# A fused token block on Trainium2: the normalised final rows written by ScalarE straight into the payload, and turned there by identity matmuls

## The reference, cut to what matters

```python
h = (emb2[hash2] + emb3[hash3] + emb4[hash4]) / 4          # three gathers of 64 values a token
x = layernorm(h)
h = h + x + layernorm(linear_attention(x)) @ Wo + bo       # phasor features, running sums over the sequence
xf = layernorm(h)                                          # the "final rows"
node = 0
for level in range(8):                                     # a tree of 255 nodes, per token
    score = xf . w1s[node] + b1s[node]
    out += (xf @ w2s[node] + b2s[node]) * gelu(abs(score))
    node = 2 * node + 1 + (score > 0)
return h + out
```

## Time and profile before

| what | us |
|---|---|
| median of 3 runs | 322.69 (322.09 to 326.11) |
| profiled execution, its own time | 326.45 |
| its span in the profile | 324.5 |
| busy, PE / DVE / ACT / POOL | 217.1 / 206.7 / 144.7 / 220.8 |
| mean granted clock of TensorE | 0.847 of 2.4 GHz |

### The profile page before, as it was taken

How to read it: one execution, slowest core, us unless ns; L and a number is a source line. 1 busy time by engine, 2 the same in 40 slices (tenths; PEclk the granted TensorE clock), 3 DMA queues, 4 the chain that set the end, 5 groups by cost and what they waited for, 6 DMA issues and landing times.

```text
span 324.5 us, 6230 instructions
## 1 busy us (share of the span) xinstructions
PE 217.1 (67%) x1973; PEld 144.8 (45%) x1978; DVE 206.7 (64%) x864; ACT 144.7 (45%) x309; POOL 220.8 (68%) x217
## 2 busy tenths in 40 slices
PE   1300555687585887586625959999999999986230
PEld 1200253546363755364412434666666667655120
DVE  5915163849596979697995502857888877864050
ACT  0003657466565657567102015545665665610230
POOL 5777777777777777777246665107877778775774
PEclk9999959557969569969975875999999999999555
DMA  4116252434334331111001122222531010102400
GB/s 140 20 28 235 54 208 48 180 73 151 110 114 117 102 89 28 38 49 51 17 33 41 49 79 89 63 98 78 146 109 15 13 17 12 16 14 65 132 7 3
DMA packets 12574, 23.80 MB, mean 73 GB/s; under 512 B 6213, under 2 KB 8452, under 8 KB 11581
## 3 DMA queue, kind: packets, MB, share of 16 engines
q1 hardware_dynamic: 4478, 16.92, 15.4%
q0 software_dynamic: 8064, 6.49, 9.6%
HBM read 17.09 MB, written 7.40 MB: 75 GB/s over the span
## 4 chain that ended last, share of the span: by engine, by line
POOL 30%; PE 25%; issue 19%; DVE 16%; DMA 5%; ACT 4%; DVEq 0%; POOLq 0%; SPq 0%; ACTq 0%
POOL pages L316 22%; PE sc L760 7%; POOL out L355 5%; PE mm L657 3%; POOL out L362 3%; ACT xb L453 2%; DMA pages<-emb,idx 2%; PE hs L718 2%; DMA pages<-slots 2%; PE yp L734 2%; PE mm L734 1%; DVE bn L937 1%; DVE xfin L980 1%; DVE gr L1137 1%; PE hs L636 1%
## 5 line engine op out<-in xcount | busy, mean ns | idle before, releaser
L316 POOL DMA_INDIRECT pages<-emb,idx x96 | 95.3, 992 | 32.5 <-issue 28.4
L355 POOL DMA_INDIRECT out<-pages,roi x64 | 70.1, 1096 | 34.8 <-issue 19.2
L323 POOL DMA_INDIRECT slots<-xov,idx x32 | 32.0, 1001 | 21.0 <-DVE idx L929 12.5
L760 PE MATMUL sc<-scratch,wf 128*64 128x204 f32 (+2 forms) x448 | 41.7, 302 | 0.0
L1102 DVE TENSOR_TENSOR scratch<-mm,feat 128x408 f32<-128x408 f32 x38 | 22.0, 579 | 13.0 <-PE sc L760 8.8
L760 PEld LDWEIGHTS sc<-scratch,wf 128*64 128x64 f32 (+1 forms) x448 | 24.7, 136 | 9.6 <-issue 5.0
L1102 DVE TENSOR_TENSOR scratch<-yp,feat 128x408 f32<-128x408 f32 x38 | 22.0, 579 | 6.5 <-PE yp L734 6.4
L1129 DVE SCALAR_TENSOR_TENSOR g<-s,cw,ge 128x102 f32<-128x102 f32 x20 | 6.4, 318 | 21.8 <-ACT ge L469 21.8
L657 PE MATMUL mm<-sel,tri 128*128 128x512 bf16 x65 | 19.0, 446 | 0.7 <-issue 0.6
L552 PE MATMUL mm<-cw,feat 128*128 128x128 f32 x32 | 8.0, 398 | 16.9 <-ACT feat L404 16.9
L453 ACT COPY xb<-xq 64x408 f32<-64x408 f32 x19 | 9.3, 489 | 21.4 <-PE xq L705 21.4
(11 more groups left out here) (227 smaller groups left out, 572.3 us busy)
## 6 DMA issues: line engine op xcount, KB each, us to landing
wf<-nodes SPq DMA_DIRECT2D x3, 1376.0 KB
slots<-wf SPq DMA_DIRECT2D x2, 1657.5 KB, 6.0
pages<-slots SPq DMA_DIRECT2D x8, 414.4 KB
wov<-turns SPq DMA_DIRECT2D x16, 176.0 KB
pages<-emb,idx POOLq DMA_INDIRECT x96, 2.4
wf<-nodes SPq DMA_DIRECT2D x1, 1312.0 KB
cw<-small SPq DMA_DIRECT2D x1, 1031.5 KB, 4.8
out<-pages,roi POOLq DMA_INDIRECT x64
```

Of the source, the lines that this page charges most:

```text
L316: pool.indirect_dma_start(emb[:, t, j, :], None, table, bass.IndirectOffsetOnAxis(idx[:, j, t:t + 1], 0)).then_inc(g_emb[g], 16)
L323: pool.indirect_dma_start(slots, bass.IndirectOffsetOnAxis(idx1[:, t:t + 1], 0), pay[:, t, :], None, bounds_check=SLOTS - 1, oob_is_err=Fa ...
L355: pool.indirect_dma_start(rows_out, bass.IndirectOffsetOnAxis(roi[:, n:n + 1], 0), xs[:, n, D:TOKEN], None, bounds_check=B * T - 1, oob_is ...
L760: last = pe.matmul(zps[half(h), page(first - 2 * h, count)], weights, z[0:rows, c, page(first, count)], start=(c == 0), stop=(n in final))
```

## The change

The tile `xfin` is gone. DVE no longer forms the normalised final rows; it hands over `ryf`, a copy of the four columns of `ry`, and `nbf` = -mean x ry. ACT's `payload` writes the rows itself, with four activations of 128x64 in place of one copy of 128x256. PE's `turn_h` waits for ACT's payload (`a_pay`) and no longer for DVE (`d_xf`), reads the rows from the payload (stride of 130 values per tile), and turns each tile by an fp32 matmul with the identity as the moving operand: four matmuls, 64 columns of weights each, instead of two transposes of 128 columns.

```diff
@@ sb tiles
-        nbias = sb("nbias", [P, GT])
+        nbias, nbf, ryf = (sb(n, [P, GT]) for n in ("nbias", "nbf", "ryf"))
-        xfin = sb("xfin", [P, GT, D])
@@ ACT, payload(g)
                 act.wait_ge(d_xf, g + 1)
                 act.wait_ge(g_clear, 2)
-                act.copy(pay[:, tiles(g), 0:D], xfin[:]).then_inc(a_pay, 1)
+                for t in range(GT):
+                    ins = act.activation(pay[:, g * GT + t, 0:D], h2[:, g * GT + t, :], ACT.Identity, bias=nbf[:, t:t + 1], scale=ryf[:, t:t + 1])
+                ins.then_inc(a_pay, 1)
@@ PE, turn_h(g)
-                pe.wait_ge(d_xf, g + 1)
+                pe.wait_ge(a_pay, g + 1)
                 if g:
                     pe.wait_ge(a_fT, g)
                     pe.wait_ge(d_bits, g)
-                for p in range(HP):
-                    last = pe.transpose(hps[:, tile(p)], xfin[:, 2 * p:2 * p + 2, :].rearrange("q t d -> q (t d)"), ident)
+                for t in range(GT):
+                    last = pe.matmul(hps[half(t % 2), tile(t // 2)], pay[:, g * GT + t, 0:D], ident, start=True, stop=True)
                 last.then_inc(p_hT, 1)
@@ DVE, layernorms(a, r, f)
                     if f:
-                        dve.wait_ge(p_hT, f)
                         dve.wait_ge(a_pay, f)
-                    for t in range(GT):
-                        ins = dve.tensor_scalar(xfin[:, t, :], h2[:, f * GT + t, :], mv[:, c + t, 0:1], ry[:, c + t:c + t + 1], ALU.subtract, ALU.mult)
-                        if t < GT - 1:
-                            put(ins)
-                        else:
-                            ins.then_inc(d_xf, 1)
+                    put(dve.tensor_copy(ryf[:], ry[:, c:c + GT]))
+                    dve.scalar_tensor_tensor(out=nbf[:], in0=mv[:, c:c + GT, 0], scalar=-1.0, in1=ry[:, c:c + GT], op0=ALU.mult,
+                                             op1=ALU.mult).then_inc(d_xf, 1)
```

## The result

The changed kernel takes 338.45 us (median of 4 runs, 337.87 to 339.14); the kernel before, run beside it, 324.4 (322.09 to 326.12). The ratio is 1.0439, 95% interval 1.0351 to 1.0527. Medians here are over all runs of a kernel, while each ratio compares the fast runs of the two kernels alone, so the two can say different things by a per cent or two. The forecast was 327.3 with a range to 331.6: the direction is right, but the measured loss of 14 us is three times the forecast 4.6. Its profiled execution took 338.2 us, its span is 336.4, against 326.45 and 324.5 before. The last scatter, which stood at 180.61, stands at 193.85, so the first stage lost 13.2 us; the rest of the span even gained 1.3.

A forecast was written before the change was run, and what follows sets the result against it. POOL's gathers feed passes 0 to 7; passes 7 to 10 are one chain through DVE, ACT and PE. Passes 5 and 6 leave 0.8, passes 7 to 10 add 1.85, 0, 1.05, 0.9: +4.6 on 322.69 gives 327.3 us, range 323.6 to 331.6.

The forecast's parts named there:

- DVE: DVE's layernorms: four L980 operations go, two small ones come at 0.3 us, leaving DVE 0.6 us ahead.
- ACT: ACT's payload: four activations in 1.44 us replace a copy of 0.39, holding ACT 1.0 us longer a pass.
- PE: turn_h: four partly overlapping matmuls cost 0.2 us more than two transposes at the high clock, 0.4 at the low.
- The new wait: turn_h waits for ACT's payload behind centre: xT +1.85 us at the high clock, about +1.7 at the low.
- The slack taken from the gathers: Passes 3 to 6: gather waits hide +1.8 each in 3 and 4, and 2.64 of 3.5 in 5 and 6.
- Pass 9: Tail of the first stage: later payload and turn_h delay L636 and then the bits, +1.05 us.
- pass 10: Last pass, at the low clock: fT at 175.1 instead of 174.21, +0.9 us.
- that delay goes into hidden, tanh, L398 and L915 without cover: Chain behind xT in a pass with centre: the delay of +1.85 us (+1.7 at low clock) carries on in full.
- Pass 8: Pass without centre: attend 0.2 us later, bits earlier, projection starts within 0.1 of before, so 0.
- 8.95 assumed: Centre to xT in passes 3 to 7: delays of +1.8, +1.8, +1.7, +1.8 and +1.85 us.
- The rival that named the cause: PE idle before turn_h: passes 4 and 6 stay at low clock, 2.2 us a lost rise, 331.0 us; chance 0.24.
- Its sign: Clock rival's mark: first stage ends more than 7 us later, with PE's clock at 0.50 in passes 4 and 6.

The follow-up runs named there:

- the fill: Changed kernel with eight idle-filling products on PE ahead of turn_h's wait for the payload: 463.06 us, 1.037 of the kernel before; again 457.57, 1.020.
- without the hand-over: Kernel before with DVE writing rows into the payload, ACT's copy gone, four identity matmuls turning them behind DVE: 444.58 us, 1.001; with four fills 447.65, 0.999.
- changed_again: The changed kernel run once more, unaltered, in the second batch of experiments: 466.63 us, 1.038 of the kernel before.
- before_again: The kernel before, unchanged, run for its trace in the third batch: 441.1 us (1 run).
- act_four: Kernel before with payload by ACT's four activations, DVE still making xfin and PE's transposes kept: 459.98 us, 1.029; again 459.15, 1.021.
- wait_pay: Kernel before with one wait changed, turn_h waiting for ACT's payload copy instead of DVE's xfin: 458.16 us, 1.020 of the kernel before.
- order: Changed kernel with only ACT's and PE's order altered, turn_x ahead of payload and turn_h, node_scores last: 465.75 us, 1.037 of the kernel before.

## Why the prediction was wrong

**Right.** DVE: L980 to L986 is 0.14 us apart, the two small operations cost no more than the 0.3 assumed. ACT: four activations in 1.42, assumed 1.44. PE: +0.2 and +0.5, assumed 0.2 and 0.4, overlapping. The new wait: 3.87 us from centre to xT at the high clock, assumed 1.97 + 1.85 = 3.82. The slack taken from the gathers: 6.3 us against 3.6 + 2.64 = 6.2. Pass 9 cost 1.4 (1.05 forecast) and pass 10 0.8 (0.9): nbf and the bits are at 176.01 and 180.54, then 184.62 and 189.15, where L980 and the bits stood at 164.98 and 168.12, then 172.18 and 175.90.

**Wrong: the step "that delay goes into hidden, tanh, L398 and L915 without cover".** It carried the delay and took the stretch itself as unchanged. That stretch grew by 5.5 us over passes 3 to 7, because PE ran it at 1.2 GHz. Pass 8, put at 0, cost 1.6 (nbf at 164.69, 9.5 behind L980 of before; one pass later 11.0): there the clock was low, and the projection took 1.92 us for 1.08 in the kernel before:

```profile
170.26 1.92 PE L645 MATMUL yp<-wpd,yT 128*128 128x256 f32 x4
```

Together this is 7.1 of the 8.6 us by which the first stage's +13.2 exceeds the +4.6 of the forecast. Of the rest, 1.2 are centre to xT (+10.1 against 8.95 assumed): in passes 3 and 4 it took 4.60, which is +2.6 and +2.5 where +1.8 was assumed, again at the low clock, while pass 5 added 0.5 less than assumed; and 0.3 are pass 9.

**The rival that named the cause, with the wrong size and occasion.** I named the clock, at 0.24 and 331.0, as a rise lost through a pause of 1.3 us. Its sign came true: the first stage ends more than 7 us later, with the granted clock at 0.50 in passes 4 and 6. But 331.0 is 7 us short of what was measured. A pause of 1.3 is that of a pass in which the clock is low and the increments end late: in pass 3, which begins at the low clock, it is 1.0. With the clock high they end early, and in passes 4 to 7 the pause is 3.1 to 3.5 us. So the fast passes made the longest pause, the clock fell in it or behind it, and the work behind it was slow: not a rise that fails once or twice but a fall that comes back pass after pass. The windows show it: 0.00 us busy in 114 to 116, and a granted clock of 1.00, then 0.82, then 0.50. "TensorE: Matmul & The Clock Gate", Part 1, of the Trainium skill says that idling throttles the clock, and these windows agree. I had quoted it for its direction only and not worked out the pause for both clocks.

**What settled it.** With the fill xT to the end of the phases takes 6.12 or 6.13 in nine passes of ten, and the total falls by 9.1 in the batch that holds both kernels; without the hand-over nothing measurable is lost. Of the 16.6 us between the traces of changed_again and before_again (113.3 - 96.7), 10.3 are the hand-over in passes 3 to 7 and 6.0 the clock in their phases; the remaining parts nearly cancel. Left open: why act_four and wait_pay lose their clock in some passes and not in others, why order loses it in all without a long pause, and what the totals of the experiments hold besides the first stage.

## What to carry to other kernels

Before moving work to an engine "that has time", ask what stands behind it in that engine's order, and which other engine's order waits for that: here 1.4 us of ACT, an engine with a busy share of 45%, stood in the one chain that set the pass. Work out the pause that a new wait makes on TensorE for both clocks, and price the matmuls behind it at 1.2 GHz too; the fast case has the longer pause. Read the clock over the stretch that sets the pass and not over the whole span. By the rows, the changed pipeline would still just hide under its gathers if the clock stayed high (0.2 + 3.87 + 6.13 + 5.46 = 15.7 us a pass, 16 us a gather); with two more microseconds for the low clock it does not.

## What the runs showed of the hardware

Filling an idle TensorE with eight useless 128x512 matmuls a pass made the same kernel 9.1 us faster in one batch (466.63 to 457.57); some 5 us of this show in the first stage of the two traces.

The same stretch of work, xT to the end of the phases, took 6.12 to 6.14 us with the granted clock at 1.00 and up to 8.26 us at 0.56 to 0.66. The mean granted clock of the whole span did not show the difference: it is 0.847 in both kernels, and one is 4.4% slower.

The same program took 324 us in the first comparison and 446 to 451 in the batches of the experiments, with engines at rest for over 40 us in pass 1; the comparison of kernels still came out alike, +14 us for the change in the one and +15.9 in the other.
